# Position scores written straight into the score ring and shifted in place

## What is computed

```python
AC = jnp.einsum('bhid,bhjd->bhij', q + u_bias[None, :, None, :], k)
BD = jnp.einsum('bhid,hjd->bhij', q + v_bias[None, :, None, :], rp)   # rp: 2*Lq - 1 positions
BD = _rel_shift(BD)                                                   # row i shifted by its own i
attn = jax.nn.softmax((AC + BD) * scale, axis=-1)
out = jnp.einsum('bhij,bhjd->bhid', attn, v)
```

## Time and profile before

| | |
|---|---|
| time, median of 3 runs | 3520.98 us (3506.55 to 3529.43) |
| span of the profiled execution | 3513.5 us |
| mean granted TensorE clock | 0.930 |
| busy: PE, ACT, DVE, POOL | 87%, 74%, 71%, 68% |
| DMA data | 668.86 MB, mean 190 GB/s |
| queue of the moves | 327680 packets, 537.92 MB, 71.5% of 16 engines' span |

### The profile page before, as it was taken

The page is one execution under the profiler, slowest core; times in us unless marked ns, Lnnn a source line. Parts: engine busy times, 40 slices in busy tenths (PEclk is TensorE's granted clock), DMA queues, the critical chain, the costliest instruction groups (busy, mean ns, idle before and its releaser), DMA issues. The chain is left out here.

```text
span 3513.5 us, 113065 instructions
## 1 busy us (share of the span) xinstructions
PE 3066.5 (87%) x40768; PEld 2088.1 (59%) x40768; DVE 2487.6 (71%) x4784; ACT 2583.4 (74%) x4106; POOL 2393.8 (68%) x4232
## 2 busy tenths in 40 slices
PE   5565399999999999988989999999999998999965
PEld 2444166666666666666666666666666666666645
DVE  2546177787677777777868777777777776777766
ACT  2333378888788888777878888887888887888842
POOL 3224668787677878876868788777777787777720
PEclk8777599999999999999999999999999999999987
DMA  5323798998999999998999999999999999999851
GB/s 184 102 90 112 204 188 204 197 213 200 191 207 199 215 214 211 207 200 174 214 195 212 202 213 212 200 207 193 209 206 212 201 212 191 204 206 203 196 165 53
DMA packets 463823, 668.86 MB, mean 190 GB/s; under 512 B 294960, under 2 KB 386992, under 8 KB 396208
## 3 DMA queue, kind: packets, MB, share of 16 engines
q0 software_dynamic: 327680, 537.92, 71.5%
q1 hardware_dynamic: 135600, 123.75, 13.9%
HBM read 77.48 MB, written 46.14 MB: 35 GB/s over the span
## 5 line engine op out<-in xcount | busy, mean ns | idle before, releaser
L650 POOL DMA_DIRECT2D score<-to_move x4096 | 2262.0, 561 | 735.9 <-PE pt_bank L832 600.0
L889 ACT COPY to_move<-pos_bank 128x512 f32<-128x512 f32 x2048 | 1087.7, 610 | 538.5 <-PE pos_bank L765 352.5
L899 ACT ACTIVATE score<-score,low 128x1024 f32<-128x1024 f32 x1024 | 1213.5, 1186 | 20.0 <-DVE low L950 11.7
L832 PEld LDWEIGHTS pt_bank<-ident_sb,score 128*128 128x128 f32 x8192 | 965.8, 143 | 307.8 <-DVE prob_t L959 78.5
L832 PE MATMUL pt_bank<-ident_sb,score 128*128 128x128 f32 x8192 | 1129.8, 280 | 18.9 <-issue 11.7
L950 DVE CUSTOM_DVE_ANT_0 score<-ac_bank,score 128x1024 f32<-128x1024 f32 x512 | 626.9, 1224 | 651.4 <-PE ac_bank L818 582.4
L959 DVE COPY prob_t<-pt_bank 128x512 f32<-128x512 f32 x1536 | 1008.1, 684 | 7.6 <-PE pt_bank L832 6.7
L765 PE MATMUL pos_bank<-pos,qv 96*32 96x512 bf16 (+15 forms) x12160 | 651.7, 322 | 115.9 <-DMA qv<-qv_parts 51.7
L950 DVE CUSTOM_DVE_ANT_0 score<-ac_bank,score,low 128x1024 f32<-128x1024 f32 x512 | 656.5, 1282 | 129.1 <-PE ac_bank L818 108.0
L846 PE MATMUL acc_bank<-prob_t,vs 128*32 128x128 f32 x16384 | 682.1, 283 | 23.2 <-issue 23.1
L818 PE MATMUL ac_bank<-ks,qu 96*128 96x512 bf16 x2048 | 635.4, 392 | 9.4 <-DVE low L950 5.8
(11 more groups left out here) (94 smaller groups left out, 939.7 us busy)
## 6 DMA issues: line engine op xcount, KB each, us to landing
score<-to_move POOLq DMA_DIRECT2D x4096, 128.0 KB, 6.4
pos<-pos_parts SPq DMA_DIRECT2D x96, 128.0 KB, 9.2
ks<-k_parts SPq DMA_DIRECT2D x192, 64.0 KB, 7.3
qu<-qu_parts SPq DMA_DIRECT2D x768, 16.0 KB, 7.8
qv<-qv_parts SPq DMA_DIRECT2D x576, 16.5 KB, 5.1
v_heads<-v_sb SPq DMA_DIRECT2D x8, 1024.0 KB, 7.3
vs<-v_heads SPq DMA_DIRECT2D x32, 256.0 KB, 10.1
pos_parts<-part SPq DMA_DIRECT2D x16, 384.0 KB, 3.0
```

The costliest lines, as they stand in the source:

```text
L650: pool.dma_start(score[s::QUAD, dst:dst + FT, :], to_move[s::QUAD, src:src + FT, QUAD - 1 - s:QUAD - 1 - s + L])\
L832: last = pe.matmul(PT[c % 2][:, t * P:(t + 1) * P], lhsT=score[:, slot(k), c * BANK + t * P:c * BANK + (t + 1) * P], rhs=ident_sb[:, :], i ...
L889: act.copy(to_move[:, at + f, c * BANK:(c + 1) * BANK], ring(m)[:, :]).then_inc(pos_out, 1)
L899: act.activation(cols, cols, ACT.Exp, bias=low[:, slot(k), NH - 1:NH], scale=-1.0)\
```

## The change

`to_move` goes away. `score` becomes a ring of four groups (`RING`) with rows 2080 wide. ACT copies the items straight into it; its wait before a group's first copy is now that the group four back in the ring has been turned. GpSimd's DMAs read and write the same rows: two tiles that lie side by side in a row's memory are taken as one run of 2080 + 2048 = 4128 elements (16,512 bytes) that is shifted down by 31 - s places. Row set s = 31 needs no shift and gets no DMA, so there are 31 DMAs a group (`MOVES`), each of four rows by two runs where there were four rows by four runs of 2048 elements (8,192 bytes). GpSimd waits for the group's 17 items alone. The order of the bodies, and everything on TensorE, stays.

```diff
--- before.py
+++ after.py
@@ -530,7 +530,8 @@
             CLUSTER = 4
             MOVE_ORDER = [CLUSTER * c + i for i in range(CLUSTER) for c in range(QUAD // CLUSTER)]
             FT = 4
-            SRC, DST, HALVES = 2, 3, 2
+            RING = 4
+            MOVES = QUAD - 1
             NK, NH = L // BANK, 2
             HALF = L // NH
             TILES, GROUPS = HEADS * NI, HEADS * NI // FT
@@ -542,11 +543,10 @@
             GQ = FT * P
             QVW = GQ + 16
             PSL = 4
-            assert FIRST + STEPS * NT < TILES - 3 * NI // 2 and NT % (FT * DST) == 0 and NT % (2 * PAIR) == 0
+            assert FIRST + STEPS * NT < TILES - 3 * NI // 2 and NT % (FT * RING) == 0 and NT % (2 * PAIR) == 0
 
             low = s2("low", [P, 16, NH])
-            to_move = s2("to_move", [P, SRC * FT, MWIN])
-            score = s2("score", [P, DST * FT, L])
+            score = s2("score", [P, RING * FT, MWIN])
             qu = [s2(f"qu{i}", [STACK, GQ], BF16) for i in range(2)]
             qv = [s2(f"qv{i}", [STACK, QVW], BF16) for i in range(2)]
             ks = [s2(f"ks{u}", [STACK, L], BF16) for u in range(2)]
@@ -567,7 +567,7 @@
             pos_loaded = [sem(f"head_pos_loaded{u}") for u in range(2)]
             vs_loaded = [sem(f"vs_loaded{u}") for u in range(2)]
             output_stored = [sem(f"output_stored{u}") for u in range(2)]
-            moved = [sem(f"moved{i}") for i in range(DST)]
+            moved = [sem(f"moved{i}") for i in range(RING)]
             pos_full, pos_out = sem("pos_full"), sem("pos_out")
             ac_full, added, exped = sem("ac_full"), sem("added"), sem("exped")
             turned, weighed = sem("turned"), sem("weighed")
@@ -611,11 +611,11 @@
                 done, names = (copied_act, BY_ACT) if (k % FT, c) in BY_ACT else (copied, BY_DVE)
                 eng.wait_ge(done, group(step, k // FT) * len(names) + (names.index((k % FT, c)) + 1))
 
-            def use_of_dst(step, j):
-                return step * (NT // FT // DST) + j // DST
+            def use_of_ring(step, j):
+                return step * (NT // FT // RING) + j // RING
 
             def slot(k):
-                return k % (DST * FT)
+                return k % (RING * FT)
 
             MADE_AT = (range(0), range(0, 6), range(6, 12), range(12, ITEMS))
             FOLD_AT = MADE_AT[1].stop
@@ -640,22 +640,25 @@
 
             @block.gpsimd
             def _(pool):
+                def pairs_of_tiles(rows, first):
+
+                    return rows.rearrange("p (i f) w -> p i (f w)", f=2)[:, :, first:first + MWIN + L]
+
                 def move(step, j):
 
                     wait_apart(pool, pos_out, group(step, j) * ITEMS + ITEMS)
-                    if there(step, FT * (j - DST)):
-                        wait_apart(pool, turned, tile(step, FT * (j - DST + 1)) * NK)
-                    src, dst = j % SRC * FT, j % DST * FT
+                    at = j % RING * FT
                     for s in MOVE_ORDER:
-                        pool.dma_start(score[s::QUAD, dst:dst + FT, :],
-                                       to_move[s::QUAD, src:src + FT, QUAD - 1 - s:QUAD - 1 - s + L])\
-                            .then_inc(moved[j % DST], 16)
-                for j in range(DST):
+                        if s < QUAD - 1:
+                            pool.dma_start(pairs_of_tiles(score[s::QUAD, at:at + FT, :], 0),
+                                           pairs_of_tiles(score[s::QUAD, at:at + FT, :], QUAD - 1 - s))\
+                                .then_inc(moved[j % RING], 16)
+                for j in range(RING):
                     move(0, j)
                 with pool.Fori(0, STEPS) as step:
-                    for j in range(DST, DST + NT // FT):
+                    for j in range(RING, RING + NT // FT):
                         move(step, j)
-                for j in range(DST, GROUPS - STEPS * (NT // FT)):
+                for j in range(RING, GROUPS - STEPS * (NT // FT)):
                     move(STEPS, j)
 
             @block.sync
@@ -881,14 +884,14 @@
 
                 def take(step, j, m):
 
-                    if m == 0 and group_there(step, j - SRC):
-                        act.wait_ge(moved[(j - SRC) % DST], use_of_dst(step, j - SRC) * (16 * QUAD) + 16 * QUAD)
+                    if m == 0 and group_there(step, j - RING):
+                        act.wait_ge(turned, tile(step, (j - RING + 1) * FT) * NK)
                     act.wait_ge(pos_full, group(step, j) * ITEMS + (m + 1))
-                    at, f, c = j % SRC * FT, m // NK, m % NK
+                    at, f, c = j % RING * FT, m // NK, m % NK
                     if m < ITEMS - 1:
-                        act.copy(to_move[:, at + f, c * BANK:(c + 1) * BANK], ring(m)[:, :]).then_inc(pos_out, 1)
+                        act.copy(score[:, at + f, c * BANK:(c + 1) * BANK], ring(m)[:, :]).then_inc(pos_out, 1)
                     else:
-                        act.copy(to_move[:, at:at + FT, L:MWIN],
+                        act.copy(score[:, at:at + FT, L:MWIN],
                                  ring(m)[:, 0:FT * QUAD].rearrange("p (f w) -> p f w", w=QUAD)).then_inc(pos_out, 1)
 
                 def exponential(step, k, h):
@@ -942,7 +945,7 @@
                 def add(step, k, h):
 
                     if h == 0 and k % FT == 0:
-                        dve.wait_ge(moved[k // FT % DST], use_of_dst(step, k // FT) * (16 * QUAD) + 16 * QUAD)
+                        dve.wait_ge(moved[k // FT % RING], use_of_ring(step, k // FT) * (16 * MOVES) + 16 * MOVES)
                     if h:
                         dve.wait_ge(added, tile(step, k) * NH + h)
                     wait_apart(dve, ac_full, tile(step, k) * NH + (h + 1))
```

## The result

The changed kernel takes 3417.74 us (median of 4 runs, 3409.44 to 3438.59) against 3525.2 (4 runs). The ratio is 0.9729, 95% interval 0.9674 to 0.9783: 2.7% faster. I had forecast 3316 us, 5.8% faster. The time lies inside the stated range, but the gain is 107 us where 205 were forecast.

The account below looks back on a forecast made before the run. It took TensorE and the DMA engines to be near their limits, with source-buffer reuse stalling the kernel. 124 groups at 21.7 us plus 53.1 saved 195.8 us, with the start 204.5: 3521 became 3316 us, range 3255 to 3445.

Parts of the forecast that it names:

- TensorE's floor: Attention stage: a group of four tiles takes TensorE 21.35 us without a stall; some 230 us in all are lost above it.
- It is the source buffer's reuse that stalls the kernel: ACT's copies wait for moves to free `to_move`, 182.0 us in 49 pieces, and TensorE runs dry behind them.
- every other term is under 10 us: Only the DMA rate with moves queued, about 215 GB/s, could upset the forecast; all else was put under 10 us.
- Part (a): ACT writes positions straight into the score ring: no added cost, and its 182.0 us of waits and following clock drops go.
- rival 3: The wait moves to the vector engine's additions and is as bad there: 22.3 us a group, 3391 us; chance 0.09.
- Part (b): GpSimd no longer waits for `turned` before a group's moves: counted at zero, at best 2 us more slack.
- Part (c): 31 moves with longer runs, 2.4% fewer bytes: a group takes 21.7 us, near the 215 GB/s row; 195.8 us less.
- Rival 2: Transfers bound the stage at their present mean rate, 203.9 GB/s: 22.7 us a group, 3435 us; chance 0.18.
- signs given for being right: Changed profile: no ACT waits for moves, groups about 21.7 us apart, clock near 1.0, 210 to 215 GB/s, 31 x 128 moves.
- Part (d): At the start the first addition waits for the first group's moves alone, at 415.5 instead of 424.22: 8.7 us gained.
- port rule: Moves touch two of 16 SBUF ports each; four at a time give 218 GB/s, 21.2 us a group, so TensorE sets the pace.

Follow-up runs that it names:

- old_wait: The changed kernel with ACT again waiting, before a group's first copy, for the moves of the group two back; 3443.34 us, ratio to the kernel before 0.9800.
- all_32: The changed kernel with the 32nd move too, which copies the unshifted rows onto themselves; 3417.31 us, ratio to the kernel before 0.9734.
- capped: The changed kernel with GpSimd issuing each part of four moves only when the part two before has landed, at most eight outstanding; 4452.55 us.

## Where the prediction failed and where it held

- *What bounds the kernel.* TensorE's floor of 21.35 us was right: the kernels with fewer moves run at 21.4. The sentence that failed is "It is the source buffer's reuse that stalls the kernel". It was one cause of two, with 52 to 69 of the 124 us of TensorE's gaps; 55 to 72 were behind fetches. The sum has no term for the fetches; "every other term is under 10 us" put at nothing what measures 82.5 us in the changed kernel, without the lower clock behind it. I had worked from the waits that name a releaser; the rows with "issue" (23.1, 20.3 and 11.7 us for TensorE's matmuls before) I didn't follow, and the queue `q8 instruction` I didn't look at.
- *Part (a).* ACT's waits went as forecast and the vector engine has slack, so rival 3 didn't happen. But ACT's 182.0 us were not TensorE's: TensorE's own gaps behind ACT's copies were 52 to 69 us. And the wait was worth 26 us by itself; with it (`old_wait`) the gaps behind fetches are 51.4 us, without it 82.5.
- *Part (b).* GpSimd's wait at zero: 11 us alone, with intervals that overlap, so right as far as the runs tell. Undone together with the other parts, it and the 32nd move cost 36 us; which of the two, no run shows.
- *Part (c)* is the mis-sized term: 22.55 us a group instead of 21.7, 105 of the 112.6 us by which the profiled span (3421.6) missed 3309. The rates I took it from came out as expected: over 30 stretches with moves being issued 214 GB/s (215 before), over 30 between them 192 (182 before). The step from there to a group's length was wrong: nothing waits for the moves, so their rate doesn't set the pace; 4.62 MB in 22.55 us are 205 GB/s because the group takes 22.55 us, and the median group ran at 21.40. Of the signs given for being right, ACT's waits, the 3968 moves and a clock near 1.0 (0.98 between 600 and 3000 us) came; groups about 21.7 us apart and 210 to 215 GB/s in the stage (206) did not. Rival 2 gave 3435 and came nearer than the forecast, by luck: additions that wait for moves in most groups, which it needs, aren't there. That the measured time lies inside the stated range is no merit of the mechanism either.
- The 2.4% of bytes saved are worth nothing by themselves: `all_32` moves them and takes 3417.31 us.
- *Part (d)*, the start: 2.7 us gained instead of 8.7. The first addition starts at 421.5. I had followed ACT's wait alone; TensorE stood before the third group's positions for its `qv` load, until 409.72 us before and until 412.08 now:

```profile
412.08 2.90 PE L768 MATMUL pos_bank<-pos,qv 96*32 96x512 bf16 x28 [12.80 <-DMA qv<-qv_parts]
```

- Of the port rule of the Trainium skill ("SBUF — State Buffer", section "Door 1: The DMA port swizzle"): the estimate of 218 GB/s was near the 214 measured with moves being issued, and TensorE's floor, which it gave as the bound, is the floor of most groups; whether all would reach it with every fetch in time no run shows. The Trainium skill's rule on whole packets ("DMA: Bandwidth & Descriptors", section "Queues, rings and completion order": a DMA engine finishes one before it serves another queue) speaks for what was seen with runs of 33 KB, 105.8 us of gaps behind fetches against 82.5; the runs of 8 KB with 92.9 speak against it as the whole story.
- Sum for the changed kernel: 149 us above the floor (2849.6 less 124 x 21.35 and 53.1), of which 82.5 are gaps behind fetches, 5.8 the turning of the loop and at most 46 the half clock of 92 us. Some 15 us stay unexplained. The kernel before has 239 us above the floor: 123.7 of gaps, 7.8 of the loop and at most 96 of half clock. So of the 90 us between them, 41 are gaps that went and about 50 the clock that no longer fell behind them.

## What to carry to other kernels

In this long unrolled program the instruction fetches share the DMA engines with the data. When the engines' busy share is near 1, look for gaps with no releaser inside a run of matmuls, and for packets of the instruction queue that land just before they end. A wait that goes frees only what the next limit leaves: price it by the idle time and the clock of the engine at its floor, not by the waiting engine's own, and look at every other row of idling, those without a name too. Try a kernel with part of the traffic left out first; here the kernel with 24 of 31 moves gives the price of full DMA engines, 135 us.

## What was unexpected in the hardware

- Late instruction fetches: TensorE goes on 1.5 us (median) after a 16 KB fetch has landed; 2 late at 174 GB/s and a DMA share of 0.76, 52 at 206 GB/s and 0.98, 64 at 204 GB/s and 0.95 with runs of 33 KB.
- The turning of a loop on TensorE came with a stop of 2.8 to 3.2 us at DMA shares of 0.35 to 0.76, and of 5.8 and 7.8 us in the changed kernel and the one before, at 0.98 and 0.96 (once in each kernel).
- SP's time to issue one 16 KB load is 0.42 us (median) at 75 GB/s and 1.4 us at 206 GB/s.
- A run of 16 semaphore increments on TensorE's own queue leaves it idle for 1.3 us (median), and its clock then drops: 256 of them a group take the group from 21.4 to 47.0 us.
- The rate of these transfers grows with the number outstanding: 152 GB/s with four or five (`capped`), 216 with eight to eleven (changed kernel).
